# Cross attention with 16 dims per head: two heads' scores in bands of 32 rows, four heads turned per unit, normalisation moved to the output

## The chip, the cores and the metric

The kernel runs on one core of one Trainium2 chip. A core has a matmul engine (TensorE, PE in the profile; PEld is its weight load), a vector engine (VectorE, DVE), an activation engine (ScalarE, ACT), a general engine (GpSimd, POOL) and a queue for DMAs (SyncE, SP). Each engine runs its own list of instructions in order and waits on semaphores for the others. Matmuls write to PSUM, which has 8 banks of 2 KB in each of 128 partitions; everything else lies in SBUF. The metric is the device time of one execution in microseconds (us).

## The reference

Four small transformers are chained over the same stream x of shape (8, 112, 256): blocks of self attention, cross attention to a context of 375 tokens, and feed-forward layers (one of them a mixture of 8 experts). The change concerns the two cross attentions whose heads have 16 dims, in the first and the second transformer. Each of them computes, per batch element:

```
q = heads(norm(x) @ wq + bq)      # 16 heads x 112 x 16
k = heads(ctx @ wk + bk)          # 16 heads x 375 x 16
v = heads(ctx @ wv + bv)
s = einsum('bhqd,bhkd->bhqk', q, k) / 4
a = softmax(s, axis=-1)
o = einsum('bhqk,bhkd->bhqd', a, v)
x = x + merge(o) @ wo + bo
```

Everything is float32. The first transformer normalises the context as well.

## The kernel before

The program is a row of thirteen blocks. A cross block of this kind (`L0_ca`, `L1_ca`) works through the 8 batch elements. Ahead of the first element stands a prologue that makes its q, k and v; then comes one body per element, and a tail for the last one. The bodies of elements 1 to 6 are a loop over pairs. A body has 16 steps, and each step is one head, called a unit. In the body of element b the engines also make q, k and v of element b+1, in eight pieces: XT turns the normalised x, CT0 and CT1 turn the context, then come Q, K0, K1, V0 and V1. `SCHEDULES` gives, by hand, at which step PE does each piece (`plan`), at which step DVE and POOL do their parts (`dve`, `pool`), how many steps a head's probabilities are turned after its scores (`lag`), at which step the previous element's output is projected (`out_step`), and which PSUM banks the pieces, the scores and the turned probabilities use. A piece goes from PE to PSUM, and ACT takes it out to SBUF; ACT does so in its own list, behind the step's exponentials.

What happens to one head:

- `scores` (L683) multiplies q, masked to this head's 16 rows, with k: contraction over all 128 rows, 112 columns of weights, 375 moving columns. Two banks alternate. The masked q comes from `spread_q` on POOL (L497), eight masked copies for each half of the heads.
- `maxima` (L1243) takes the negative row maximum on DVE.
- `exps` (L975) writes exp(s - max) to one of four buffers in SBUF and sums the rows.
- `reciprocals` (L1248) inverts the sum on DVE; `scale` (L1530) multiplies the probabilities by it on POOL.
- `turn` (L696) transposes the 112 x 375 probabilities in three pieces of 125 columns on PE, `copy_turned` (L1257) copies them to SBUF on DVE.
- After four heads, `weigh` (L723) multiplies them with v: twelve matmuls whose weights are 32 columns wide, each head in its own 32 columns of the array.
- After sixteen heads, `evacuate` (L983) adds the value bias on ACT, `project` (L746) multiplies by wo, and `update` (L1289, L1290) adds the result to x.

One float32 matmul appears as two MATMUL records in the profile, one transposition as one.

## Time and profile before

| | us |
|---|---|
| median of 3 runs | 2317.31 |
| lowest and highest run | 2315.89, 2319.47 |
| the profiled execution, its own time | 2322.28 |
| its span, first to last instruction | 2320.4 |

The page of the profile gives for the whole span: PE busy 86%, its weight load 63%, DVE 70%, ACT 38%, POOL 36%. The two blocks in question lie at 139 to 375 us (`L0_ca`) and at 911 to 1145 us (`L1_ca`), together 20% of the span. The rest belongs to blocks that the change doesn't touch. Since the share of busy time is a mean over stages with different limits, the two blocks have to be read for themselves: the windows view gives busy time by stretch, and the view of instructions in order of time shows what follows what.

### The profile page before, as it was taken

To read this page: it belongs to the slowest core of one execution; us is meant where nothing else is said; L and a number is where in the kernel's file an instruction comes from. 1 tells how busy PE (TensorE), PEld (TensorE's weight loads), DVE (VectorE), ACT (ScalarE), POOL (GpSimd) and SP (SyncE) were. 2 spreads that over 40 slices of the span, in tenths; PEclk is the share of its full clock that TensorE was granted. 3 is DMA by queue.
4 is the path that set the end of the run, shared out by engine and by line. 5 is a ranking of instruction groups with operands and counts; after the bars stand their busy time and mean duration, and the time that the engine had idled before them with its cause. 6 is when DMAs were issued, how large, how long until landed. Compare 5 with 4: busy or idle time off the path is not lost.

```text
span 2320.4 us, 35838 instructions
## 1 busy us (share of the span) xinstructions
PE 2002.0 (86%) x11112; PEld 1464.4 (63%) x11112; DVE 1619.0 (70%) x3586; ACT 891.3 (38%) x2427; POOL 830.1 (36%) x950
## 2 busy tenths in 40 slices
PE   5879997999996877999888999685886968898878
PEld 4657776889895656777665555473444745565557
DVE  5856767677776876666665676595775958777765
ACT  4545553222222643555424444222331234444421
POOL 2235554666662233555420010041000424444433
PEclk9989998999997988999889999896997979999979
DMA  4100000211101000000100010101001000000100
GB/s 176 33 14 15 13 0 1 101 73 37 52 41 68 1 1 7 15 25 31 59 7 14 14 61 0 45 1 55 0 0 65 1 1 11 20 10 10 64 1 16
DMA packets 21631, 67.18 MB, mean 29 GB/s; under 512 B 880, under 2 KB 18568, under 8 KB 18832
## 3 DMA queue, kind: packets, MB, share of 16 engines
q1 hardware_dynamic: 21520, 65.78, 8.0%
q8 instruction: 59, 0.97, 0.2%
q14 instruction: 52, 0.43, 0.1%
HBM read 64.83 MB, written 0.95 MB: 28 GB/s over the span
## 4 chain that ended last, share of the span: by engine, by line
PE 60%; DVE 23%; issue 10%; ACT 3%; POOL 2%; DMA 1%; DVEq 0%; SPq 0%; POOLq 0%; ACTq 0%
PE ps L809 11%; PE ps L848 9%; PE ps L683 9%; PE ps L643 5%; PE ps L648 4%; PE ps L746 4%; PE ps L696 4%; PE ps L728 3%; PE ps L678 3%; POOL arena L1530 2%; PE ps L723 2%; PE ps L635 2%; DVE g_split_sb L1378 2%; DVE arena L1240 1%; DVE arena L1432 1%
## 5 line engine op out<-in xcount | busy, mean ns | idle before, releaser
L1530 POOL TENSOR_TENSOR arena<-arena,rinv 112x375 f32<-112x375 f32 (+1 forms) x448 | 372.0, 830 | 579.6 <-DVE rinv L1248 571.8
L683 PE MATMUL ps<-arena 128*112 128x375 f32 (+1 forms) x1280 | 387.5, 410 | 20.0 <-ACT arena L975 13.2
L809 PE MATMUL ps<-h_split_sb,w_split_sb 128*128 128x448 f32 x1536 | 355.5, 376 | 5.3 <-DVE h_split_sb L1368 4.3
L1559 POOL TENSOR_TENSOR w_split_sb<-wml,ones 128x256 fp32r<-128x256 f32 (+1 forms) x104 | 106.5, 1024 | 608.0 <-PE ps L809 396.6
L809 PEld LDWEIGHTS ps<-h_split_sb,w_split_sb 128*128 128x128 f32 x1536 | 298.4, 195 | 33.5 <-issue 5.9
L696 PEld LDWEIGHTS ps<-cst,arena 112*125 112x125 f32 (+1 forms) x1408 | 216.1, 183 | 156.5 <-POOL arena L1530 56.7
L848 PE MATMUL ps<-g_split_sb,w_split_sb 128*128 128x448 f32 x1248 | 292.9, 372 | 21.5 <-DVE g_split_sb L1378 21.1
L1243 DVE TENSOR_REDUCE negmax<-ps 112x1 f32<-112x375 f32 (+1 forms) x288 | 159.3, 553 | 159.2 <-PE ps L683 158.8
L848 PEld LDWEIGHTS ps<-g_split_sb,w_split_sb 128*128 128x128 f32 x1248 | 232.7, 189 | 55.6 <-DVE g_split_sb L1378 36.8
L975 ACT ACTIVATE arena<-ps,negmax 112x375 f32<-112x375 f32 (+1 forms) x384 | 190.5, 501 | 190.3 <-DVE negmax L1243 189.4
L696 PE MATMUL ps<-cst,arena 112*125 112x112 f32 (+1 forms) x1408 | 229.5, 275 | 38.6 <-POOL arena L1530 38.2
L683 PEld LDWEIGHTS ps<-arena 128*112 128x112 f32 x1280 | 176.7, 182 | 65.6 <-issue 24.6
L1377 DVE CAST g_split_sb<-arena 128x448 fp32r<-128x448 f32 x208 | 133.7, 643 | 112.6 <-PE ps L848 91.6
L975 ACT ACTIVATE arena<-arena,negmax 112x112 f32<-112x112 f32 (+1 forms) x256 | 125.8, 492 | 173.1 <-DVE negmax L1243 173.1
L1378 DVE TENSOR_TENSOR g_split_sb<-arena,g_split_sb 128x448 fp32r<-128x448 f32 x208 | 186.0, 894 | 7.1
L1257 DVE COPY arena<-ps 125x336 f32<-125x336 f32 x384 | 187.6, 488 | 2.3 <-PE ps L696 1.7
L643 PE MATMUL ps<-wat,arena 128*125 128x256 f32 (+1 forms) x704 | 175.7, 387 | 2.3 <-ACT arena L924 1.7
L1033 ACT ACTIVATE arena<-ps,wml 128x448 f32<-128x448 f32 x128 | 81.5, 637 | 233.6 <-PE ps L809 229.6
L643 PEld LDWEIGHTS ps<-wat,arena 128*125 128x125 f32 (+1 forms) x704 | 127.1, 188 | 33.9 <-issue 15.5
L746 PE MATMUL ps<-wat,arena 128*112 128x256 f32 x512 | 130.1, 402 | 14.6 <-DVE arena L1282 11.1
L1565 POOL TENSOR_TENSOR w_split_sb<-wml,ones 128x256 fp32r<-128x256 f32 x104 | 70.0, 673 | 194.5 <-PE ps L848 194.5
L1280 DVE RECIPROCAL arena<-ps 128x448 f32<-128x448 f32 x32 | 94.5, 2952 | 57.8 <-PE ps L734 57.8
(159 smaller groups left out, 3014.1 us busy)
## 6 DMA issues: line engine op xcount, KB each, us to landing
wml<-in_wm_L_moe SPq DMA_DIRECT2D x8, 2052.0 KB, 8.2
craw<-in_ctx SPq DMA_DIRECT2D x40, 375.0 KB
wml<-in_wm_L_m SPq DMA_DIRECT2D x3, 3072.0 KB, 14.0
wat<-in_wa_L_ca SPq DMA_DIRECT2D x2, 2560.0 KB, 9.4
wml<-in_wm_L_m SPq DMA_DIRECT2D x2, 2048.0 KB, 9.7
arena<-gates_hbm SPq DMA_DIRECT2D x1, 3584.0 KB, 11.0
wat<-in_wa_L_sa SPq DMA_DIRECT2D x1, 2560.0 KB, 8.8
wat<-in_wa_L_sa SPq DMA_DIRECT2D x2, 1024.0 KB, 9.6
```

The costliest lines, as they stand in the source:

```text
L643: last = mm(ps[0:blk.kp, W_BANK, i * D:(i + 1) * D], kv[:, k2, q * blk.kp:(q + 1) * blk.kp], w[:, k2], start=k2 == 0, stop=k2 == DC - 1)
L683: last = mm(ps[0:S, S_BANK + s % blk.s_banks, i * blk.nk:(i + 1) * blk.nk], qz[:, parity(b), head_of(u) if blk.dh == 16 else u], kT[:, par ...
L696: last = nc.tensor.transpose(ps[0:blk.kp, T_BANK + s % blk.t_banks, o:o + S], buf[:, i * blk.nk + q * blk.kp:i * blk.nk + (q + 1) * blk.kp ...
L746: last = mm(ps[0:S, blk.out_bank, 0:D], oT[:, c], wo[:, c], start=c == 0, stop=c == blk.cq - 1)
L809: last = mm(out, w[:, k2, v], h_split_sb[:, h, k2, tokens], start=k2 == 0 and i == 0, stop=k2 == DC - 1 and i == 2)
L848: last = mm(ACC(c, half), w[:, c * P:(c + 1) * P], g_split_sb[:, half, g], start=f == 0 and i == 0, stop=f == FC - 1 and i == 2)
L975: last = go(probs[0:S, s % blk.nprobs, i * nk:(i + 1) * nk], src[:, i * nk:(i + 1) * nk], ACT.Exp, bias=negmax[:, u:u + 1], accum_out=rows ...
L1243: v.tensor_reduce(negmax[:, s * blk.heads:(s + 1) * blk.heads], src, AX_X, ALU.max, negate=True).then_inc(maxed, 1)
L1257: last = v.tensor_copy(pT[0:kp, g % 4, :, s % HG], T_[:, 0:KC * S].rearrange("p (k s) -> p k s", s=S))
L1377: link(v.tensor_copy(g_split_sb[:, t % 2, 0], g32[:, t % 2]))
L1378: v.tensor_tensor(g_split_sb[:, t % 2, 1], g32[:, t % 2], g_split_sb[:, t % 2, 0].bitcast(F32), ALU.subtract)\
L1530: pool.tensor_tensor(p3, p3, r3, ALU.mult).then_inc(scaled, 1)
```

## The change

In both cross blocks with 16 dims per head (`blk.rows`):

- Scores. Two masked copies of q take the place of sixteen: one keeps the even group of 16 rows in each 32, the other the odd one (`maskz`). A head's scores are then a contraction over 32 rows, and `scores_of_rows` issues those of two heads, in two bands of 32 rows and to two banks, every second step. Four banks take scores where two did.
- `maxima_of_rows` reduces two heads with one instruction; eight take the place of sixteen.
- The probabilities stay unscaled. `scale` on POOL and fifteen of the sixteen `reciprocals` go. Eight buffers hold them where four did.
- `turn_rows` turns one third of four heads at a time (four transpositions of 125 columns into one bank), on three of every four steps; `keep_rows` copies 125 x 448. Twelve such units take the place of sixteen.
- `weigh` comes 10 steps after the head's step where it came 4 steps after.
- Normalisation at the output: `invert_rows` inverts the sixteen sums at once, `widen_shares` (POOL) spreads them to 16 columns each, `share` turns the result with two transpositions on PE, `keep_shares` copies it on ACT, `share_out` multiplies the output by it on DVE, `add_value_bias` adds the bias on POOL. They take the place of `evacuate`.
- The plan: the pieces move to other steps, and all of them go through PSUM bank 7 (`w_banks=[7]`), where three banks took turns. `out_step` goes from 6 to 11, `lag` from 3 to 6. `cnorm`, the context's norm in `L0_ca`, moves from step 2 to step 1 of DVE's list.

```diff
     "L0_ca": dict(
-        plan={2: ["XT"], 4: ["CT0"], 8: ["CT1"], 10: ["Q"], 12: ["K0"], 13: ["K1"], 14: ["V0"], 15: ["V1"]},
-        dve={0: ["norm"], 2: ["cnorm"]},
-        pool={12: ["spread0"], 14: ["spread1"]},
-        out_step=6, lag=3, s_banks=2, t_banks=2, w_banks=[7, 3, 2], out_bank=7),
+        plan={1: ["XT"], 2: ["CT0"], 3: ["CT1"], 5: ["Q"], 7: ["K0"], 9: ["K1"], 13: ["V0"], 15: ["V1"]},
+        dve={0: ["norm"], 1: ["cnorm"]},
+        pool={7: ["spread"]},
+        out_step=11, lag=6, s_banks=4, t_banks=2, w_banks=[7], out_bank=7),
...
+                def scores_of_rows(b, s):
+                    wait(pe, exped, count(st["unit"], units, b, s - 2))
+                    if s == 0:
+                        pe.wait_ge(spread, count(st["spread"], 1, b, 1))
+                        wait_evacuated(pe, blk, st, b, ["K0", "K1"])
+                    c, z = s // 8, s // 4 % 2
+                    for i in (s % 4, s % 4 + 1):
+                        rows = slice(32 * i, 32 * i + 32)
+                        mm(ps[0:S, S_BANK + i, 0:blk.nk], qzr[rows, parity(b), z, c], kT[rows, parity(b), c, 0:blk.nk],
+                           start=True, stop=True).then_inc(scored, 1)
+
+                def turn_rows(b, g, q):
+                    pe.wait_ge(exped, count(st["unit"], units, b, 4 * g + 4))
+                    wait(pe, row_kept, count(12 * st["row"], 12, b, 3 * g + q - 1))
+                    for i in range(4):
+                        last = nc.tensor.transpose(ps[0:blk.kp, T_BANK + (3 * g + q) % 2, i * S:(i + 1) * S],
+                                                   probs8[0:S, 4 * (g % 2) + i, q * blk.kp:(q + 1) * blk.kp], ident[0:S, 0:S])
+                    last.then_inc(row_turned, 1)
+
+                def share(b):
+                    pe.wait_ge(row_wide, count(st["row"], 1, b, 1))
+                    for c in range(DC):
+                        last = nc.tensor.transpose(ps[:, O_BANK, (DC + c) * S:(DC + c + 1) * S],
+                                                   rwide[:, parity(b), c * P:(c + 1) * P],
+                                                   ident[0:S, 0:S])
+                    last.then_inc(shares_full, 1)
...
+                        if at and blk.rows and at[1] % 4 < 3:
+                            turn_rows(at[0], at[1] // 4, at[1] % 4)
...
+                        due = lagged(b, s, WEIGH_AFTER, units)
+                        if blk.rows and due and due[1] % 4 == 0:
+                            weigh(due[0], due[1] // 4)
+                            if due[1] // 4 == 3:
+                                share(due[0])
...
+                    if blk.rows:
+                        act.wait_ge(row_maxed, count(8 * st["row"], 8, b, s // 2 + 1))
+                        wait(act, row_turned, count(12 * st["row"], 12, b, 3 * (s // 4 - 1)))
+                        go(probs8[0:S, s % 8, 0:nk], ps[0:S, S_BANK + s % 4, 0:nk], ACT.Exp, bias=negmax[:, s:s + 1],
+                           accum_out=rowsum[:, parity(b), s:s + 1]).then_inc(exped, 1)
+                        return
...
+                def keep_shares(b):
+                    act.wait_ge(shares_full, count(st["row"], 1, b, 1))
+                    go(shares, ps[:, O_BANK, DC * S:2 * DC * S], ACT.Copy).then_inc(shares_kept, 1)
...
+                def maxima_of_rows(b, s):
+                    dve.wait_ge(scored, count(st["unit"], units, b, s + 2))
+                    v.tensor_reduce(negmax[:, s:s + 2], ps[0:S, S_BANK + s % 4:S_BANK + s % 4 + 2, 0:nk], AX_X, ALU.max, negate=True)\
+                        .then_inc(row_maxed, 1)
...
+                def share_out(b):
+                    dve.wait_ge(shares_kept, count(st["row"], 1, b, 1))
+                    v.tensor_tensor(oT[:, 0:DC].rearrange("p c s -> p (c s)"), ps[:, O_BANK, 0:DC * S], shares, ALU.mult)\
+                        .then_inc(o_shared, 1)
...
-                        scale(b, s)
+                        if not blk.rows:
+                            scale(b, s)
```

Where it moves things, at two places of the loop body. PE's list of `L0_ca` before, at steps 3 to 5 (L683 scores, L696 turn, L723 weigh, L623 the piece CT0):

```order
259 L683 MATMUL ps<-arena 112x375 [waits exped]
260 L696 MATMUL ps<-cst,arena 125x112 [waits turned,scaled]
261 L696 MATMUL ps<-cst,arena 125x112 x2
262 L723 MATMUL ps<-arena,vz 32x112 [waits turned]
263 L723 MATMUL ps<-arena,vz 32x112 x11
...
269 L618 REGISTER_ALU [waits w_done1]
270 L623 MATMUL ps<-cst,arena 128x125 [waits cn_ready]
```

The same list after the change, at steps 2 and 3 (L707 scores of two heads, L715 turn, L768 weigh, L631 the pieces CT0 and CT1):

```order
238 L707 MATMUL ps<-arena 112x375 [waits exped]
239 L707 MATMUL ps<-arena 112x375
...
241 L715 MATMUL ps<-cst,arena 125x112 [waits row_kept]
242 L715 MATMUL ps<-cst,arena 125x112 x3
...
245 L768 MATMUL ps<-arena,vz 32x112 x11
...
247 L626 REGISTER_ALU [waits w_done0]
248 L631 MATMUL ps<-cst,arena 128x125 [waits cn_ready]
...
250 L715 MATMUL ps<-cst,arena 125x112 [waits row_kept,exped]
...
253 L631 MATMUL ps<-cst,arena 128x125 [waits cn_ready,w_done0]
```

CT1 now follows CT0 by one unit of turning, and waits for the bank that CT0 is in (`w_done0`); before, four steps and another bank lay between.

DVE's list of `L0_ca` before, at steps 2 and 3 (L1243 maxima, L1248 reciprocals, L1257 copies, L1116 the context's norm):

```order
259 L1243 TENSOR_REDUCE negmax<-ps 112x1 [waits scored]
260 L1248 RECIPROCAL rinv<-rowsum 112x1 [waits exped]
261 L1257 COPY arena<-ps 125x3x112 [waits av_done,transposed]
...
265 L1116 TENSOR_SCALAR arena<-craw,ctx_mean,ctx_rstd_ln 125x256
...
271 L1243 TENSOR_REDUCE negmax<-ps 112x1 [waits scored]
```

The same list after, at steps 0 to 2 (L1315 maxima, L1320 the sixteen reciprocals, L1326 copies, L1184 both norms):

```order
210 L1315 TENSOR_REDUCE negmax<-ps 112x2 [waits scored]
...
212 L1320 RECIPROCAL rinv<-rowsum 112x2x2x4 [waits exped]
...
215 L1326 COPY arena<-ps 125x448 [waits av_done]
...
219 L1184 TENSOR_SCALAR xn<-X,mv,rstd 112x256
...
223 L1184 TENSOR_SCALAR arena<-craw,ctx_mean,ctx_rstd_ln 125x256
...
229 L1315 TENSOR_REDUCE negmax<-ps 112x2 [waits scored]
```

The norm of x, the three instructions of the context's norm and the reciprocals now stand in one row between the maxima of the first two pairs of heads; before, two maxima lay between the two norms.

## Rows read from the trace of the kernel before

**Rows 1.** The page: the whole span.
```profile
span 2320.4 us, 35838 instructions
```
**Rows 2.** Windows: length; busy us of PE, PEld, DVE, ACT, POOL; granted clock; DMA.
```profile
139.80:149.60 9.80, 9.42 (x37) 7.43 (x38) 0.84 (x3) 4.48 (x10) 3.33 (x2) 0.73 0.13 39
149.60:175.90 26.30, 24.87 (x181) 17.36 (x180) 16.48 (x48) 15.17 (x43) 15.52 (x17) 1.00 0.05 16
175.90:340.90 165.00, 163.23 (x1298) 118.70 (x1297) 113.76 (x330) 93.27 (x270) 97.48 (x108) 1.00 0.03 10
340.90:370.40 29.50, 24.70 (x214) 16.98 (x212) 21.64 (x74) 12.11 (x37) 16.39 (x22) 0.94 0.01 2
912.30:921.20 8.90, 8.88 (x36) 7.40 (x37) 0.00 (x0) 4.00 (x10) 3.33 (x2) 0.76 0.14 43
947.00:1111.80 164.80, 161.94 (x1298) 117.86 (x1297) 106.67 (x312) 92.67 (x270) 97.22 (x108) 1.00 0.07 23
```
**Rows 3.** Groups by line and shape in 175.9:340.9: count, busy us, mean ns, idle before.
```profile
L683 PE MATMUL ps<-arena 128*112 128x375 f32 x193 | 80.4, 497 | 1.8 <-ACT arena L975 1.3
L975 ACT ACTIVATE arena<-ps,negmax 112x375 f32<-112x375 f32 x96 | 55.1, 574 | 57.5 <-DVE negmax L1243 57.1
L1243 DVE TENSOR_REDUCE negmax<-ps 112x1 f32<-112x375 f32 x96 | 52.2, 544 | 47.7 <-PE ps L683 47.6
L1257 DVE COPY arena<-ps 125x336 f32<-125x336 f32 x96 | 46.8, 487 | 0.0
```
**Rows 4.** PE in order of time, L0_ca: start, duration to the last end, line, shape.
```profile
241.51 0.48 PE L696 MATMUL ps<-cst,arena 112*125 112x112 f32 x3
241.91 0.78 PE L723 MATMUL ps<-arena,vz 125*32 125x112 f32 x24
242.63 0.88 PE L683 MATMUL ps<-arena 128*112 128x375 f32 x2
243.35 0.48 PE L696 MATMUL ps<-cst,arena 112*125 112x112 f32 x3
...
243.99 0.80 PE L683 MATMUL ps<-arena 128*112 128x375 f32 x2
244.62 0.48 PE L696 MATMUL ps<-cst,arena 112*125 112x112 f32 x3
```
**Rows 5.** PE in order of time, L3_ca: 448 columns, weights 64 wide, two heads together.
```profile
2071.35 2.48 PE L728 MATMUL ps<-arena,vz 125*64 125x448 f32 x12
```
**Rows 6.** Groups by line and shape, whole span: DVE copies 448 columns out of PSUM.
```profile
L1259 DVE COPY arena<-ps 112x448 f32<-112x448 f32 x64 | 38.5, 601 | 4.2 <-PE ps L696 4.0
```
**Rows 7.** ACT in order of time, prologue of L1_ca: CT0 and CT1, Q.
```profile
913.64 1.06 ACT L926 ACTIVATE arena<-ps 128x375 f32<-128x375 f32 x2
915.90 0.60 ACT L914 ACTIVATE qs<-ps,cst 128x112 f32<-128x112 f32 x2 [1.20 <-PE ps L628]
```
**Rows 8.** The tail of L0_ca in order of time: last scores, last project.
```profile
364.50 0.80 PE L683 MATMUL ps<-arena 128*112 128x375 f32 x2
...
370.40 2.04 PE L746 MATMUL ps<-wat,arena 128*112 128x256 f32 x4 [0.72 <-ACT arena L983]
```
**Rows 9.** DVE in order of time, L0_ca: norm of x, norm of the context.
```profile
232.78 0.72 DVE L1116 TENSOR_SCALAR xn<-X,mv,rstd 112x256 f32 x1
235.32 1.32 DVE L1116 TENSOR_SCALAR arena<-craw,ctx_mean,ctx_rstd_ln 125x256 f32<-125x256 f32 x3
```
**Rows 10.** PE in order of time, L3_ca: two idle times, then 512 columns.
```profile
2064.55 0.41 PE L613 MATMUL ps<-cst,xn 112*128 112x112 f32 x2 [1.07 <-DVE xn L1115]
...
2066.80 3.67 PE L648 MATMUL ps<-wat,arena 128*112 128x512 f32 x4 [0.89 <-ACT arena L918]
...
2073.75 1.97 PE L648 MATMUL ps<-wat,arena 128*112 128x512 f32 x4
```
**Rows 11.** Windows of L3_ca, columns as in rows 2.
```profile
2062.90:2066.80 3.90, 1.94 (x11) 1.32 (x10) 3.83 (x10) 1.89 (x6) 1.62 (x2) 1.00 0.44 136
2066.80:2070.50 3.70, 3.70 (x5) 1.52 (x6) 1.88 (x6) 0.70 (x2) 0.81 (x1) 0.54 0.00 1
```

More of the change, by code:

```diff
@@ L177, in starts @@
             at["unit"] += B * blk.units
[L178 to L179 removed]
+            at["turn"] += B * blk.units * (not blk.keys_first and not blk.rows)
+            at["row"] += B * blk.rows
+            at["spread"] += B * blk.rows
             at["pair"] += B * 2 * blk.keys_first
```

117 lines of the change are left out of this document (86 added, 31 removed).

## The prediction

> **What bounds the kernel now.** The windows come first, since the two blocks that change are a fifth of the span [rows 1]. For each of them they separate a prologue, a first body, six steady bodies and the last body with its tail [rows 2]. In the steady stretch of L0_ca PE is busy 163.2 of 165.0 us at the full granted clock, DVE 113.8, ACT 93.3, POOL 97.5. L1_ca reads the same: 161.9 of 164.8. So a body of 27.5 us (165.0 / 6) is bound by PE, and POOL's multiplications, though many, wait for others. Next comes PE in order of time [rows 4]. The reader is to take pitches there, from one start to the next, since a matmul's end is modelled. A head's scores take 0.63 us (243.99 to 244.62), or 0.72 where the 32-column matmuls stand ahead of them (242.63 to 243.35). Three transpositions take 0.32 us (243.35 to 243.67, the row left out there being CT0), or 0.40 when those matmuls follow (241.51 to 241.91). Four groups of four 32-column heads are not drawn out: 24 records of 112 columns pass in 0.72 us (241.91 to 242.63).
>
> **PE, per steady body.** Out go the scores of 16 heads, 12 at 0.63 and 4 at 0.72: 10.4 us, 10.7 with the short waits in the loop's first steps. In come 8 pairs, whose price the trace doesn't hold, since nothing runs in bands of rows yet. Its bounds: side by side, a pair streams for as long as one head, 0.63 us; one after the other, for 1.26 us. To either belongs the passage between forms. From full width into 32-column tiles costs 0.40 - 0.32 = 0.08 us; out of them, the last groups' pitch and the slow first load cost about 0.09 + 0.09 us [rows 4]. A pair has a passage in, 112 columns to load that nothing hides (0.09, the 0.72 against 0.63), and a passage out with the next load open: about 0.36 us. So a pair costs between 0.63 (all of it hidden) and 1.62 us, and I take 0.63 + 0.36 = 1.0 us. The reason is the nearest row: in L3_ca two heads in 64-column halves pass 12 records of 448 columns in 2.40 us, 0.20 us each, where a head's score record of 375 columns alone takes 0.315 us, which is 0.376 us for 448 [rows 4, 5]. Halves of columns run side by side at 0.20 / 0.376 = 0.53, almost two at once, though each matmul's two records follow each other in the list. Bands of rows are the same kind of split. Eight pairs at 1.0 make 8.0 us: a gain of 2.7.
>
> The Trainium skill (TensorEngine Tiling (Array Packing), Key Properties) says that changing the tiling mode drains the engine. The 0.08 us in and the 0.09 us out agree, for columns; no row here shows it for bands. The same skill (TensorE: Matmul & The Clock Gate, Measured speedup vs the span model) has four bands reach 3.07 times, and by that two would come close to two.
>
> The 48 transpositions remain: 0.107 us each (0.32 / 3). With four passages into the weighing it is 5.5 us before and after. Weighing keeps its matmuls, but each of its four ends now falls on transpositions with an open load, 4 x 0.09 = 0.4 us more; before, that stood in the 0.72 of the scores. `share` adds two transpositions, 0.25 us. The waits on exponentials at the loop's start go, since four score banks take the place of two: a gain between 0 and 0.6 us, I take 0.3. Sum: -2.7 + 0.4 + 0.25 - 0.3 = -2.35, a body of 25.1 us if no engine makes PE wait.
>
> **The others, per body.** DVE has 8 maxima of 750 elements. 375 take 0.544 us; copies of 336 and 448 take 0.487 and 0.601, so an element more costs 1.02 ns, and 750 take 0.544 + 0.38 = 0.93 [rows 3, 6]. Its 12 copies of 448 cost 0.60 [rows 6] for 16 of 0.487 [rows 3]; the reciprocals shrink to one. `share_out` costs about 0.4. DVE falls from 19.0 (113.8 / 6) to about 16: -1.3 for the maxima, -0.6 for the copies, about -1.2 for the reciprocals (their overlap taken off), +0.4. ACT keeps 16 exponentials of 0.574, swaps one evacuation for another: no change. POOL loses 16 multiplications; its spread of q is one instruction of 448 elements. None of this bounds, so what POOL loses is worth nothing in the bodies; PE's work hides it.
>
> **The new wait.** All pieces go through bank 7, and XT, CT0 and CT1 stand at steps 1, 2 and 3. I lay the body's start out, with 0 at the first pair's start. In L1_ca: first maxima 1.05 to 2.0, two exponentials to 3.1, XT out of the bank at 3.8. DVE meanwhile does reciprocals, a copy and the norm of x (0.72) [rows 9] up to 3.3, and only then the maxima of the second pair, to 4.2. Exponential 2 ends at 4.8, and behind it in ACT's list CT0 leaves the bank at 5.3. PE arrives at CT1 at 4.65 and waits 0.7 us; queued behind it are the next pair and a turn. In L0_ca the context's norm (1.32) [rows 9] stands ahead of the second maxima too. They end at 5.4, CT0 leaves at 6.6, and PE waits about 2.0 us, 0.6 of it for `cnorm` itself. After that no wait of the hand-laid body bites: the exponentials of a group are 2 to 3 us ahead of its turning, and the bias on POOL (o_done) is 2 us ahead of `project`. Bodies: 25.1 + 0.7 = 25.8 in L1_ca, 25.1 + 2.0 = 27.1 in L0_ca. Six of each: 6 x (27.5 - 25.8) = 10.2 and 6 x (27.5 - 27.1) = 2.4 us of gain.
>
> **The edges.** In the prologue, 9.8 and 8.9 us [rows 2], the pieces overlapped over three banks. Now each of seven waits until ACT has taken the one before out: 0.53 for each context half, 0.60 for Q [rows 7], and so on, with about 0.15 until a matmul's end is seen. 7 x 0.75 = 5.3, to which cold clock adds a little and from which what was exposed already (XT) goes: +5.5 us per block, between 4 and 8. POOL's spread, 3.3 us before [rows 2], was hidden behind K and V and its saving is worth nothing. First body: no weighing of an element before, four banks: -1.8 in L1_ca, -1.0 in L0_ca. Last body and tail: 29.5 us from its first scores to the last `project` (340.9 to 370.4), the last 5.9 of them behind the start of the last scores [rows 8]. The tail grows: the last four heads go through three turns and copies, weighing, `share`, ACT, DVE and POOL, about 3 us more than one turn, one copy and ACT. The body has no pieces, so DVE leads there, with some 3 us less to do; laid out by hand the same way it comes to 28.3. That is -1.2 us per block.
>
> **The sum.** L1_ca: -10.2 - 1.8 - 1.2 + 5.5 = -7.7. L0_ca: -2.4 - 1.0 - 1.2 + 5.5 = +0.9. I add 0.8 for register work around the new waits that the hand-laid body leaves out: -6.0 us. The profiled execution took 2322.3 us (its span 2320.4), which becomes 2316.3; it lies 5.0 above the median of the runs, so the forecast is 2317.3 - 6.0 = **2311.3 us**. The span of this case: each 0.1 us on a pair is worth 128 pairs x 0.1 = 12.8 us over both blocks, so it reaches from 2298 to 2322.
>
> **Rivals.**
> *The passage costs nothing.* If weights of a band load while the other computes, a pair costs 0.8 us: -0.2 x 128 = -26 us, **2286**. For it: bands need not share rows with the load that comes next. Against: the 0.08 and 0.09 of the column tiles [rows 4].
> *The waits at CT0 and CT1 slow the clock (slower than before).* In L3_ca PE idles 1.07 and 0.89 us within 3.9 us [rows 10, 11], and the 512 columns behind that run at the lower of the two clocks (granted 0.54): 3.67 us for what takes 1.97 at full clock, +1.7. L0_ca's new wait has the same form: 2.0 us idle in about 4, with transpositions around it. Seven bodies x 1.7 = 12, and as much again in waits where ACT is behind: -6 + 12 = +6, **2323**, up to 2338. It decides from about 1 us of idle in L1_ca, 2 in L0_ca. For it: every granted-clock row of both blocks is 1.00 only because PE never waits. Against: in both blocks PE's idle time would come in two parts, around CT0, and each is shorter than 1.4 us.
> *The pair doesn't run side by side.* Each head's two records go one after the other: 1.62 per pair, +0.62 x 128 = +79 us, **2391**. Against it: rows 5, at 0.53.
> Of POOL's 97.5 us per stretch nothing comes back in any of these.
>
> **How the numbers follow.** Forecast 0.45, free passage 0.17, slow clock and waits 0.29, no pair 0.09. About 0.2% (4.6 us) is what a measurement of this kernel can tell from no change. Of the forecast's 0.45 I give 0.25 to faster, 0.14 to the band, 0.06 to slower, since its size hangs on the pair's price; of the slow clock 0.06 to the band and 0.23 to slower. Faster 0.25 + 0.17 = 0.42; same 0.20; slower 0.06 + 0.23 + 0.09 = 0.38. The range goes from 2288, the free passage but for its far end, to 2338, the top of the waits; beyond it lie the missing pair and tails, under 0.2.
>
> **What would show it.** In the changed profile: pitch from a pair's start to the turn behind it of 1.0 us (0.8: free passage; 1.6: no pair). Idle of PE ahead of the CT pieces, ended by ACT, of 0.7 us a body in L1_ca and 2.0 in L0_ca. A maximum of 0.93. Prologue of 15 us in place of 9.8. Steady stretches of about 155 us (L1_ca) and 163 (L0_ca), at granted clock 1.00. A clock under 1.00 there, or PE waiting for maxima or row_kept in the middle of a body, would make the prediction wrong; so would a change in any other block.

## The result: 3.8% slower, most of it at TensorE's lower clock

The changed kernel took 2407.56 us (median of 4 runs, 2394.78 to 2430.24), the kernel before 2318.39 us beside it (4 runs). The ratio is 1.038, with a 95% interval of 1.0336 to 1.0425. The forecast was 2311.3 us with a range of 2288 to 2338. So the sign was wrong, and the time lies far outside the range. The profiled execution took 2419.89 us, its span is

```profile
span 2418.0 us, 34738 instructions
```

against the 2320.4 of [rows 1]: 97.6 us more. I cut both spans at the turning of x (XT) of elements 0, 1 and 7 and at the last `project` of each block. The table has the lengths in us, and those of some experiments below.

| | before | after | e1 | e6 | e8 |
|---|---|---|---|---|---|
| L0_ca, XT of element 0 to XT of element 1 | 12.6 | 22.5 | 20.9 | 10.9 | 11.7 |
| L0_ca, six bodies, to XT of element 7 | 164.1 | 184.1 | 157.5 | 157.7 | 165.9 |
| L0_ca, to the last `project` | 53.8 | 58.1 | 54.9 | 49.2 | 52.8 |
| L1_ca, XT of element 0 to XT of element 1 | 13.2 | 22.2 | 20.6 | 9.8 | 9.6 |
| L1_ca, six bodies, to XT of element 7 | 164.4 | 203.5 | 154.5 | 154.9 | 161.2 |
| L1_ca, to the last `project` | 51.4 | 62.2 | 54.9 | 48.6 | 52.2 |

After against before: 18.9 us went into the two prologues, 59.1 into the bodies, 15.1 into the ends, and 4.5 outside these pieces. The windows view of the changed kernel (columns as in [rows 2]) shows what the stretches have in common:

```profile
138.40:158.60 20.20, 15.01 (x38) 8.56 (x38) 0.82 (x3) 4.51 (x10) 0.93 (x1) 0.53 0.06 20
948.40:967.00 18.60, 13.91 (x32) 7.89 (x32) 0.00 (x0) 4.02 (x10) 0.93 (x1) 0.52 0.07 21
1002.90:1208.00 205.10, 197.80 (x1315) 127.20 (x1316) 98.69 (x156) 86.21 (x265) 12.31 (x18) 0.75 0.06 18
```

The steady stretch of L1_ca ran at a granted clock of 0.75 where [rows 2] had 1.00. PE was busy for 197.8 us of it, and only 161.9 before, though it has less to do. A view of instructions in order of time, on PE, shows the point at which the clock falls in each of those bodies:

```profile
1034.14 0.89 PE L707 MATMUL ps<-arena 32*112 32x375 f32 x4
1034.95 0.69 PE L715 MATMUL ps<-cst,arena 112*125 112x112 f32 x4
1037.10 0.41 PE L621 MATMUL ps<-cst,xn 112*128 112x112 f32 x2 [1.46 <-DVE xn L1184]
1037.44 1.07 PE L707 MATMUL ps<-arena 32*112 32x375 f32 x4
1038.44 1.18 PE L715 MATMUL ps<-cst,arena 112*125 112x112 f32 x4
...
1052.63 2.66 PE L643 MATMUL ps<-arena,wat 128*128 128x375 f32 x4
1055.22 0.89 PE L707 MATMUL ps<-arena 32*112 32x375 f32 x4
```

At 1034.14 four records of scores take 0.89 us and four turns 0.69: the upper of the two levels (2.4 GHz). Then PE stands idle for 1.46 us, until the norm of x is there. The turns behind it take 1.18 us, the lower level (1.2 GHz), and it stays there until the K piece at 1052.63. After that the upper level is back, for the second half of the body, until XT comes round again. DVE in the same stretch shows why the norm is late:

```profile
1035.10 0.94 DVE L1315 TENSOR_REDUCE negmax<-ps 112x2 f32<-112x750 f32 x1 [1.10 <-PE ps L707]
1035.95 0.24 DVE L1320 RECIPROCAL rinv<-rowsum 112x16 f32<-112x16 f32 x1
1036.11 0.56 DVE L1326 COPY arena<-ps 125x448 f32<-125x448 f32 x1
1036.59 0.45 DVE L1184 TENSOR_SCALAR xn<-X,mv,rstd 112x256 f32 x1
```

DVE was free for 1.10 us. But it works its list in order, and the norm stands behind the maxima of the first pair, which wait for PE. The waits view of the six bodies of L1_ca has this one wait and no other:

```profile
PE ps L621 <- DVE xn L1184: 8.8, 6, 1.5
```

### The profile page after: what moved, and what is told of

The parts are those of the page before. It is cut to its first block, busy times and chain, and to the rows that moved or that the text cites. A ratio compares the mean times of both kernels' runs of the same rounds, so it can differ in the third digit from the quotient of the medians.

```text
span 2418.0 us, 34738 instructions
## 1 busy us (share of the span) xinstructions
PE 2064.0 (85%) x11144; PEld 1468.6 (61%) x11144; DVE 1595.4 (66%) x3170; ACT 874.8 (36%) x2411; POOL 610.9 (25%) x710
## 4 chain that ended last, share of the span: by engine, by line
PE 62%; DVE 22%; issue 10%; ACT 3%; POOL 2%; DMA 1%; DVEq 0%; SPq 0%; POOLq 0%; ACTq 0%
PE ps L863 10%; PE ps L902 9%; PE ps L715 5%; PE ps L707 5%; PE ps L651 5%; PE ps L656 4%; PE ps L791 4%; PE ps L773 3%; PE ps L688 3%; PE ps L768 2%; PE ps L643 2%; PE ps L693 2%; POOL arena L1633 2%; DVE arena L1308 2%; DVE g_split_sb L1477 2%
## 5 line engine op out<-in xcount | busy, mean ns | idle before, releaser
L1633 POOL TENSOR_TENSOR arena<-arena,rinv 112x375 f32<-112x375 f32 (+1 forms) x192 | 163.9, 854 | 388.4 <-DVE rinv L1336 388.4
L1315 DVE TENSOR_REDUCE negmax<-ps 112x2 f32<-112x750 f32 x128 | 119.9, 937 | 194.0 <-PE ps L707 193.9
L1027 ACT ACTIVATE arena<-ps,negmax 112x375 f32<-112x375 f32 x256 | 144.5, 568 | 193.9 <-DVE negmax L1315 174.8
L693 PE MATMUL ps<-arena 128*112 128x112 f32 (+1 forms) x768 | 173.3, 351 | 10.0 <-ACT arena L1011 5.5
L715 PEld LDWEIGHTS ps<-cst,arena 112*125 112x125 f32 x768 | 123.7, 232 | 87.6 <-issue 83.6
L1326 DVE COPY arena<-ps 125x448 f32<-125x448 f32 x192 | 118.3, 616 | 72.2 <-PE ps L715 70.5
L715 PE MATMUL ps<-cst,arena 112*125 112x112 f32 x768 | 157.0, 339 | 0.0
L736 PEld LDWEIGHTS ps<-cst,arena 112*125 112x125 f32 (+1 forms) x640 | 90.9, 174 | 83.5 <-POOL arena L1633 53.2
L736 PE MATMUL ps<-cst,arena 112*125 112x112 f32 (+1 forms) x640 | 104.5, 279 | 37.3 <-POOL arena L1633 37.2
L707 PE MATMUL ps<-arena 32*112 32x375 f32 x512 | 134.7, 607 | 0.0
```

The source lines that it names most:

```text
L693: last = mm(ps[0:S, S_BANK + s % blk.s_banks, i * blk.nk:(i + 1) * blk.nk], qz[:, parity(b), head_of(u) if blk.dh == 16 else u], kT[:, par ...
L707: mm(ps[0:S, S_BANK + i, 0:blk.nk], qzr[rows, parity(b), z, c], kT[rows, parity(b), c, 0:blk.nk], start=True, stop=True).then_inc(scored, 1)
L715: last = nc.tensor.transpose(ps[0:blk.kp, T_BANK + (3 * g + q) % 2, i * S:(i + 1) * S], probs8[0:S, 4 * (g % 2) + i, q * blk.kp:(q + 1) * ...
L736: last = nc.tensor.transpose(ps[0:blk.kp, T_BANK + s % blk.t_banks, o:o + S], buf[:, i * blk.nk + q * blk.kp:i * blk.nk + (q + 1) * blk.kp ...
L1027: go(probs8[0:S, s % 8, 0:nk], ps[0:S, S_BANK + s % 4, 0:nk], ACT.Exp, bias=negmax[:, s:s + 1], accum_out=rowsum[:, parity(b), s:s + 1]).t ...
L1633: pool.tensor_tensor(p3, p3, r3, ALU.mult).then_inc(scaled, 1)
```

## Experiments 1 to 4: idle time, or bands?

Two theories stood against each other. IDLE: PE's wait for XT lowers the clock. BANDS: matmuls over 32 of the 128 rows don't hold the clock up, whether PE waits or not. (In diffs and in rows of a trace, `...` stands for lines left out.) The median of the kernel before, over 11 runs beside these, was 2317.79 us.

**e1: the norm of x ahead of the first maxima on DVE.**

```diff
-                        if s == 0 and more(b) and blk.keys_first:
+                        if s == 0 and more(b) and (blk.keys_first or blk.rows):
                             extra("norm", b + 1, link)
...
-                                if name != "norm" or not blk.keys_first:
+                                if name != "norm" or not (blk.keys_first or blk.rows):
```

> The changed kernel, with the norm of x for the next element moved ahead of the first maxima in DVE's list of a body, so that PE doesn't idle 1.46 us at XT. Theory IDLE (PE's idle time at XT is what lowers the clock): granted clock of the steady bodies back to 0.97 or more, PE alternating no longer between its two levels, time 2310 to 2325 us. Theory BANDS (matmuls over 32 of 128 rows don't hold the clock, whatever the idle time): the steady bodies still spend about half their time at the lower level, and only the idle time goes, 14 x 1.5 = 20 us: about 2387 us.

Measured: 2332.1 us (6 runs), ratio 1.0061 (1.0041 to 1.0081): 7 us above the range of IDLE, and 55 below the number of BANDS. Moving one instruction of 0.40 us gave back 75 of the 89 us. On PE and in the windows view, the same place of L1_ca:

```profile
1040.86 0.69 PE L715 MATMUL ps<-cst,arena 112*125 112x112 f32 x4
1041.39 0.36 PE L621 MATMUL ps<-cst,xn 112*128 112x112 f32 x2
1041.67 0.89 PE L707 MATMUL ps<-arena 32*112 32x375 f32 x4
```

```profile
213.30:316.80 103.50, 99.88 (x875) 63.90 (x874) 68.57 (x117) 57.45 (x176) 8.29 (x12) 1.00 0.03 11
1016.00:1041.40 25.40, 25.05 (x222) 16.06 (x221) 16.25 (x27) 14.00 (x44) 2.07 (x3) 1.00 0.05 15
```

The bodies take 25.9 us (103.5 / 4) in L0_ca and 25.3 in L1_ca, at clock 1.00, with bands. So bands alone don't lower it here.

**e2: the kernel before, each head's scores over its own band of 32 rows**, one head at a time, the masked copies as they were.

```diff
+                        band = slice(32 * (u % 4), 32 * (u % 4) + 32) if blk.dh == 16 and blk.cross else slice(0, P)
                         last = mm(ps[0:S, S_BANK + s % blk.s_banks, i * blk.nk:(i + 1) * blk.nk],
-                                  qz[:, parity(b), head_of(u) if blk.dh == 16 else u],
-                                  kT[:, parity(b), u // 8, 0:blk.nk], start=True, stop=True)
+                                  qz[band, parity(b), head_of(u) if blk.dh == 16 else u],
+                                  kT[band, parity(b), u // 8, 0:blk.nk], start=True, stop=True)
```

> The kernel before, with each head's scores contracted over its band of 32 rows instead of 128 (the same masked q, one head at a time, nothing else changed). PE stays busy without idle time, each score pays the passage into and out of the band. IDLE: granted clock stays at 1.00 in the steady bodies; each head costs about 0.3 us more, 256 x 0.3 = 75 us: about 2390 us. BANDS: the clock falls to 0.85 or less in the steady bodies, and the time to 2440 us or more.

Measured: 2635.09 us (2 runs), ratio 1.1374. BANDS said 2440 us or more, and this is far above that edge; IDLE said 2390. PE in order of time in L0_ca, first at the upper level, then at a place of a later body where the level falls; and the windows view of four later bodies:

```profile
152.92 0.88 PE L684 MATMUL ps<-arena 32*112 32x375 f32 x2
153.73 0.58 PE L697 MATMUL ps<-cst,arena 112*125 112x112 f32 x3
154.24 0.88 PE L684 MATMUL ps<-arena 32*112 32x375 f32 x2
...
242.69 0.58 PE L697 MATMUL ps<-cst,arena 112*125 112x112 f32 x3
...
244.33 0.97 PE L697 MATMUL ps<-cst,arena 112*125 112x112 f32 x3
245.23 1.35 PE L724 MATMUL ps<-arena,vz 125*32 125x112 f32 x24
246.51 1.59 PE L684 MATMUL ps<-arena 32*112 32x375 f32 x2
248.03 0.97 PE L697 MATMUL ps<-cst,arena 112*125 112x112 f32 x3
```

```profile
195.50:385.90 190.40, 190.40 (x867) 105.36 (x866) 81.09 (x221) 64.09 (x180) 65.17 (x73) 0.64 0.03 9
```

PE was busy for all 190.4 us, without a single wait, and was granted 0.64. At the upper level a head and its turn take 1.32 us (0.81 + 0.51, from the pitches), against 0.95 in [rows 4]; at the lower one 2.4 (1.52 + 0.90). So a busy PE isn't enough: with one band of 32 rows at work at a time the clock falls without any idle time, again in each of these bodies.

The Trainium skill (TensorE: Matmul & The Clock Gate, Loop structure matters more than you think) says that matmuls stay at the higher clock when they are issued densely, back to back. These rows speak against that as a sufficient rule.

**e3: the changed kernel, scores over all 128 rows**, from sixteen masked copies, the layout and the late norm as changed.

```diff
-                        rows = slice(32 * i, 32 * i + 32)
-                        mm(ps[0:S, S_BANK + i, 0:blk.nk], qzr[rows, parity(b), z, c], kT[rows, parity(b), c, 0:blk.nk],
+                        mm(ps[0:S, S_BANK + i, 0:blk.nk], qz[:, parity(b), 8 * c + 2 * i + z], kT[:, parity(b), c, 0:blk.nk],
...
```

POOL spreads q to the sixteen copies, as before the change.

> The changed kernel, with sixteen masked copies of q and scores over all 128 rows, one head after the other, everything else as changed (plan, lags, banks, idle time at XT). IDLE: the clock alternates as in the changed kernel (0.68 and 0.82 in turns), the scores cost 0.3 us more a pair at full clock: 2420 to 2460 us. BANDS: granted clock 1.00 in the steady bodies in spite of the idle time, time 2335 to 2360 us.

Measured: 2372.19 us (2 runs), ratio 1.0239, 12 us above the range of BANDS and 48 below that of IDLE. The waits and windows views of L1_ca:

```profile
PE ps L621 <- DVE xn L1183: 8.1, 5, 1.6
```

```profile
1013.80:1042.70 28.90, 27.14 (x218) 19.74 (x218) 16.21 (x26) 14.19 (x45) 4.47 (x4) 1.00 0.04 15
```

The wait for XT is there, 1.6 us in each body, and the clock is 1.00 all the same. A body takes 28.9 us and not 34.2.

**e4: the kernel before, XT at step 0**, so that PE waits for the norm.

```diff
-        plan={2: ["XT"], 4: ["CT0"], 8: ["CT1"], 10: ["Q"], 12: ["K0"], 13: ["K1"], 14: ["V0"], 15: ["V1"]},
+        plan={0: ["XT"], 4: ["CT0"], 8: ["CT1"], 10: ["Q"], 12: ["K0"], 13: ["K1"], 14: ["V0"], 15: ["V1"]},
...
-        plan={3: ["XT"], 5: ["CT0"], 6: ["CT1"], 9: ["Q"], 12: ["K0"], 13: ["K1"], 14: ["V0"], 15: ["V1"]},
+        plan={0: ["XT"], 5: ["CT0"], 6: ["CT1"], 9: ["Q"], 12: ["K0"], 13: ["K1"], 14: ["V0"], 15: ["V1"]},
```

> The kernel before, with XT in step 0 of the body in both cross blocks, where it has to wait for the norm of x: 1 to 2 us of idle PE in each body, scores over 128 rows, nothing else changed. IDLE: the granted clock of the steady bodies falls to 0.9 or less, time 2360 us or more. BANDS: the clock stays at 1.00, and only the idle time is paid, 14 x 1.7 = 24 us: about 2340 us.

Measured: 2334.97 us (4 runs), ratio 1.0086. The waits and windows views of L1_ca:

```profile
PE ps L613 <- DVE xn L1116: 7.2, 5, 1.4
```

```profile
1010.00:1038.60 28.60, 26.99 (x216) 19.65 (x216) 17.89 (x52) 15.55 (x45) 16.20 (x18) 1.00 0.04 13
```

A body grows by 1.1 us, about the new wait, and the clock stays at 1.00.

Together the four give a table, for L1_ca but for e2 (L0_ca):

| scores | PE hardly waits | PE waits 1.4 to 1.6 us in a body |
|---|---|---|
| all 128 rows | 1.00 (before) | 1.00 (e3, e4) |
| 32 rows, two bands side by side | 1.00 (e1) | 0.75 (after) |
| 32 rows, one band at a time | 0.64 (e2) | not run |

Neither theory was right alone. With bands side by side the clock stays up as long as PE hardly waits, and a wait that costs the other kernels no more than itself takes it down. The price in L1_ca: a body of 34.2 us, against 25.3 in e1 plus the wait of 1.46, is 7.5 us more. In L0_ca the same wait of 1.46 us stands in every body, and they take between 28.2 and 34.3 us, where e1 has 25.9 with 0.9 of waits: 2 to 8 us beyond the wait. A pair of bands also brings two passages between forms of matmul, and none of the kernels that wait has the one without the other; e9 below separates them only for a PE that doesn't wait.

## Experiment 7: another way to take the wait away

**e7: the changed kernel, XT, CT0, CT1 and Q at steps 3, 4, 5 and 6**, in both blocks.

```diff
-        plan={1: ["XT"], 2: ["CT0"], 3: ["CT1"], 5: ["Q"], 7: ["K0"], 9: ["K1"], 13: ["V0"], 15: ["V1"]},
+        plan={3: ["XT"], 4: ["CT0"], 5: ["CT1"], 6: ["Q"], 7: ["K0"], 9: ["K1"], 13: ["V0"], 15: ["V1"]},
```

> The changed kernel with nothing but the hand layout altered: XT, CT0, CT1 and Q at steps 3, 4, 5 and 6 of the body and not at 1, 2, 3 and 5. The norm of the next element stays behind the first maxima on VectorE. Its XT was waited for 1.46 us at step 1; two steps later a pair of scores and turns of some 2.1 us lie ahead of it on TensorE. Theory IDLE: the wait of 1.46 us is what lowers the clock; with it gone the bodies come to 25.5 to 26.5 us at clock 1.00 as in e1, and the time to 2325 to 2340 us. Theory ORDER: e1 was faster for what moved on VectorE and not for TensorE's wait; then the bodies stay at 28 to 34 us and the time at 2390 us or more.

Measured: 2373.88 us (3 runs), ratio 1.0237. Both numbers missed; the bodies of L1_ca lie in the range of ORDER, the time between the two. PE in order of time in L1_ca:

```profile
1047.35 0.36 PE L621 MATMUL ps<-cst,xn 112*128 112x112 f32 x2
...
1049.08 0.54 PE L631 MATMUL ps<-cst,craw 125*128 125x125 f32 x3
1050.74 0.54 PE L631 MATMUL ps<-cst,craw 125*128 125x125 f32 x3 [1.13 <-ACT arena L980]
1051.21 1.59 PE L707 MATMUL ps<-arena 32*112 32x375 f32 x4
```

XT is no longer waited for. In its place CT1 waits 1.13 us for bank 7, which CT0 still fills, since nothing lies between the two at the new steps. The scores behind that wait are at the lower level again (1.59 for 0.89). The bodies of L1_ca come to 28.3 and 29.6 us in turn. The wait moved and the fall moved with it, which speaks for IDLE; that the loss is smaller here fits the shorter wait and the shorter stay at the lower level. In L0_ca two waits of 0.78 and 0.76 us stand in every body; two of the bodies kept granted clock 1.00 and took 27.4 us, the other three were granted 0.84 to 0.94 and took 28.9 to 31.3.

## Experiments 5 and 6: the prologue and the end

e1 still lay 14 us behind the kernel before, 11.3 in the profiled executions. The table shows 16 us in the prologues and 5 in the ends, 4 more than its bodies gain; the other 7.5 lie outside the two blocks (see e11).

**e5: e1, and the pieces of element 0 over several banks.** PE and ACT take the bank from a list of its own where `m` is 0, and PE waits for the evacuation that it needs, no longer for the last one.

```diff
+        self.first_banks = [7, 3, 2, 7, 3, 2, 7, 6] if self.rows else None
...
+                    if first:
+                        W_BANK = blk.first_banks[k]
+                        needs = {"Q": ["XT"], "K": ["CT1"], "V": ["CT1"]}.get(name[0], [])
+                        same = [j for j in range(k) if blk.first_banks[j] == W_BANK] + [blk.pieces.index(x) for x in needs]
+                        wait(pe, done, value - 1 - k + max(same + [-1]) + 1)
...
```

> The kernel of e1 (the norm ahead of the first maxima), and the eight pieces of element 0, ahead of the first body, written to banks 7, 3, 2, 7, 3, 2, 7, 6 in turn and not all to bank 7. e1 took 2332.1 us, and its stretch ahead of the first body 21.0 us in L0_ca and 20.7 us in L1_ca, against 9.8 and 8.9 us in the kernel before. Theory ONE BANK: the stretch is long because each piece waits for the evacuation of the last, and its clock is low because of those waits. Then it comes back to some 10.5 us, and the first body (28.1 us, clock 0.82) to some 26.5: 2332 - 2 x 10.4 - 2 x 1.6 = 2308 us. Theory LOW CLOCK: the clock is at its lower level there for another reason, and only the waits go (21.0 us less the 15.8 us that TensorE is busy): 2332 - 2 x 5.2 = 2322 us.

Measured: 2309.92 us (7 runs), ratio 0.996 (0.9946 to 0.9975), the kernel before at 2320.33 us beside it. First the changed kernel's prologue, PE in order of time, then that of e5:

```profile
139.92 0.86 PE L631 MATMUL ps<-cst,arena 125*128 125x125 f32 x3 [0.92 <-ACT arena L972]
141.53 0.89 PE L631 MATMUL ps<-cst,arena 125*128 125x125 f32 x3 [0.76 <-ACT arena L978]
143.18 2.05 PE L636 MATMUL ps<-arena,wat 128*128 128x112 f32 x8 [0.76 <-ACT arena L978]
145.91 2.87 PE L643 MATMUL ps<-arena,wat 128*128 128x375 f32 x4 [0.69 <-ACT qs L968]
```

```profile
140.40 1.48 PE L640 MATMUL ps<-cst,arena 125*128 125x125 f32 x6 [0.36 <-DVE arena L1195]
141.68 1.89 PE L645 MATMUL ps<-arena,wat 128*128 128x112 f32 x8
143.36 3.23 PE L652 MATMUL ps<-arena,wat 128*128 128x375 f32 x8
```

With one bank there are seven waits of 0.66 to 0.92 us, and all of the work stands at the lower level (a K piece of 2.87 us takes 1.44 in a steady body). With several banks the waits go but for one of 0.36 us, the prologue takes 9.7 us (139.43 to 149.11), and over it the granted clock is 0.74, where it was 0.53. ONE BANK was right; only the first body, which was to get 1.6 us shorter, stayed at 28.3.

**e6: e5, and the statistics for the next block taken once, at the end.** Before and after the change, DVE takes them for elements 0 to 6 in the last body, in a row of 3.5 us, and for element 7 at the very end. The end of that row in e1, on DVE, with eleven more small ones between the second and the third line, and then on PE:

```profile
356.39 0.58 DVE L1199 BATCH_NORM_AGGREGATE mv<-stat 112x2 f32<-112x6 f32 x7
357.00 0.17 DVE L1205 TENSOR_SCALAR var<-mv 112x7 f32<-112x7 f32 x1
...
359.42 0.94 DVE L1315 TENSOR_REDUCE negmax<-ps 112x2 f32<-112x750 f32 x1
```

```profile
360.94 1.11 PE L768 MATMUL ps<-arena,vz 125*32 125x112 f32 x24 [3.10 <-DVE arena L1326]
361.98 3.14 PE L715 MATMUL ps<-cst,arena 112*125 112x112 f32 x12
```

```diff
-                                statistics(tail, n + 1, 0 if b == B - 1 else B - 1, b)
+                                if not blk.rows:
+                                    statistics(tail, n + 1, 0 if b == B - 1 else B - 1, b)
+                                elif b == B:
+                                    statistics(tail, n + 1, 0, B)
```

> The kernel of e5, and the statistics of the residual for the next block taken once, for all eight elements behind the last update, and not for seven of them at step 11 of the last body and for the eighth at the end. In e1 TensorE stood idle for 3.1 us at 357.8 us, behind those statistics on VectorE, and went on at the lower clock (12 turns in 3.14 us for some 1.9). Theory TAIL: both go, in both blocks: 3.1 us of idle time, some 2 us of slow turns, weighings and projection, less some 0.5 us for seven more aggregations at the end: some 4.6 us for each block, e5 less 9 us, and 2299 us if e5 is 2308. Theory VECTORE BOUND: VectorE is the bound of the last body anyway, and only the work saved comes back (some 3 us of small instructions less 0.5, of which half is hidden): e5 less 2 to 3 us.

Measured: 2293.32 us (4 runs), ratio 0.9875 (0.9853 to 0.9898), 1.2% faster than the kernel before. The gain over e5 is 16.6 us, more than TAIL's 9. In the profiled executions the last part of a block falls from 56.0 and 54.8 us (e5) to 49.2 and 48.6, 13 in all; the whole span falls by 12.2. The twelve turns are at the upper level:

```profile
348.10 2.15 PE L724 MATMUL ps<-cst,arena 112*125 112x112 f32 x12
```

## Experiments 8 to 11: what the bands are worth, and what is not theirs

The kernel before stood at 2319.43 us over 18 runs beside these.

**e8: e6 with the scores over all 128 rows** (the diff of e3).

> The kernel of e6 (2293.3 us), with each head's scores computed over all 128 rows from 16 masked copies of the queries, as in e3: the bands alone are taken out, everything else stays. TensorE has hardly a wait in the bodies of e6 (25.3 us, clock 1.00). Theory SIDE BY SIDE: two heads in bands of their own save TensorE time at the full clock: in e3 a body was 28.9 us of which 1.6 us were the wait for XT, so 27.3 us, 2.0 us more than in e6; over 16 bodies 32 us: 2325 us. Theory CLOCK ONLY: what bands save, they lose in the first bodies and the ends, which run at the lower clock in e6 (0.82 in the first) and would not here: 2.5 us in each of two first bodies come back, and 2320 us. If the bands save nothing, it stays at 2293 us.

Measured: 2315.34 us (7 runs), ratio 0.9981 (0.9961 to 1.0), some 5 us below the lower of the two numbers. With hardly a wait in the way the bands save 22 us. A steady body takes 27.8 us in L0_ca and 27.2 in L1_ca, 1.9 more than in e6, as SIDE BY SIDE had it (2.0); the first bodies give part of that back, as CLOCK ONLY had it. The table above has 8.2 and 6.3 us of it in the bodies and 3.6 in either end; the rest lies outside the two blocks or in the spread of single executions. The first body is shorter in e8 by 1.4 us (L0_ca) and 3.0 (L1_ca), since its clock is 0.94 and 1.00 there and 0.82 in e6.

**e9: the kernel before, each head's scores over 64 rows**, as e2 but for

```diff
+                        half = slice(64 * (u % 4 // 2), 64 * (u % 4 // 2) + 64) if blk.dh == 16 and blk.cross else slice(0, P)
```

> The kernel before, with each head's scores over the 64 of the 128 rows that hold it, where e2 took 32: 2635 us at a mean clock of 0.834, and TensorE without a wait. Theory THE MORE ROWS REST, THE LOWER: the clock lies between, some 0.9, and the time at 2400 to 2500 us. Theory ONLY BANDS OF 32: 64 rows hold the full level as 128 do; then the time is that of before plus what the passages from half to full rows cost (two for each of 256 heads at some 0.05 to 0.1 us: 25 to 50 us), 2340 to 2370 us, or 2318 us if they cost nothing.

Measured: 2416.2 us (one run), in the first theory's range, but not in its way. The windows view:

```profile
183.30:247.10 63.80, 63.80 (x434) 36.42 (x433) 38.60 (x111) 31.35 (x90) 32.47 (x37) 1.00 0.04 14
967.90:1013.30 45.40, 45.40 (x214) 24.62 (x213) 18.78 (x52) 15.80 (x46) 17.28 (x20) 0.66 0.03 9
```

The steady bodies keep clock 1.00, and take 31.9 us for 27.5. That is the passages: a head and its turn take 1.32 us as in e2, against 0.95 in [rows 4], so 0.37 us for two passages, where the expectation had 0.1 to 0.2. Twelve heads a body have no weighing behind them that would bring a passage anyway: 12 x 0.37 = 4.4. Only the first body of L1_ca fell to 0.66 and took 45.4 us; a wait of 1.01 us stands 2 us ahead of it. So half the rows hold the level nearly everywhere where a quarter (e2) did not. Since a head and its turn have the same passages in both, the passages are not what takes the clock in e2.

**e10: e6 with its own plan for the first body**, CT0, CT1, Q, K0 and K1 at steps 3, 5, 7, 9 and 11.

```diff
+        self.plan0 = {1: ["XT"], 3: ["CT0"], 5: ["CT1"], 7: ["Q"], 9: ["K0"], 11: ["K1"], 13: ["V0"], 15: ["V1"]} if self.rows else self.plan
...
-                            for name in blk.plan.get(s, []):
+                            for name in (blk.plan0 if isinstance(b, int) and b == 0 else blk.plan).get(s, []):
```

> The kernel of e6, with a hand layout of its own for the first body of either attention, in which no turns lie between the pieces: CT0, CT1, Q, K0 and K1 at steps 3, 5, 7, 9 and 11 and not at 2, 3, 5, 7 and 9. In e6 TensorE waited 1.83 and 0.76 us there for CT0 and CT1, fell to the lower clock for 10 us, and the body took 28.3 us for 25.9. Theory: the waits go and with them the fall, 2.4 us in each block: 2293.3 - 4.8 = 2288.5 us. Rival: XT, CT0 and CT1 are waited for because ScalarE comes to them late, behind the exponentials, and wait again at the new steps: 2293 us.

Measured: 2297.0 us (5 runs), ratio 0.9903 (0.9888 to 0.9919): no gain over e6. The wait of 1.83 us for CT0 stayed in the first body, as the rival said; the one for CT1 fell from 0.76 to 0.34 and the body from 28.3 to 27.7. More telling is a later body of L0_ca in the profiled execution:

```profile
203.50:210.00 6.50, 5.60 (x54) 3.69 (x53) 4.92 (x10) 4.33 (x12) 0.62 (x1) 0.94 0.17 48
210.00:220.00 10.00, 10.00 (x54) 6.55 (x54) 3.03 (x5) 3.65 (x12) 0.00 (x0) 0.53 0.02 7
234.10:260.00 25.90, 25.00 (x220) 16.00 (x220) 17.11 (x30) 14.34 (x44) 2.07 (x3) 1.00 0.04 15
```

All steady bodies of L0_ca in e1, e5, e6 and e10, twenty in all, have the same two waits, 0.2 us for CT0 and 0.7 for CT1. This one fell to the lower level behind them and took 30.7 us; the one that starts at 234.1 did not. So with bands even 0.9 us of waits can be followed by a fall, once in twenty here.

**e11: the kernel before with the one edit of e6**, its statistics taken once in the two blocks.

```diff
-                                statistics(tail, n + 1, 0 if b == B - 1 else B - 1, b)
+                                if not (blk.dh == 16 and blk.cross):
+                                    statistics(tail, n + 1, 0 if b == B - 1 else B - 1, b)
+                                elif b == B:
+                                    statistics(tail, n + 1, 0, B)
```

> The kernel before, with the one edit of e6 that is not bound to the change: the statistics for the next block taken once at the end of the two cross attentions with 16 dims. Before, TensorE waits 2.95 us at 355.8 us behind them. What it gives here is to be subtracted from the gain of e6. Theory TAIL: the wait goes in both blocks, less 0.4 us of aggregations at the end: 2318 - 2 x 2.5 = 2313 us. Theory VECTORE BOUND: VectorE is the last body's bound and little comes back: 2317 us.

Measured: 2321.49 us (10 runs), ratio 1.0003 (0.9991 to 1.0016). The edit does what TAIL says inside the blocks: their ends take 49.3 and 46.9 us for 53.8 and 51.4, 9 us in all. But the profiled execution has the span of before to the tenth. The way back lies in L3_ca, which no edit touched. On DVE, in order of time:

```profile
2014.94 0.55 DVE L1240 TENSOR_TENSOR arena<-ps,mask_sb 112x375 f32<-112x375 f32 x1 [4.43 <-issue]
...
2018.14 0.35 DVE L1115 TENSOR_SCALAR xn<-X,rstd 112x256 f32 x1 [1.60 <-issue]
```

DVE stands for 4.43 and 1.60 us, and the profile names nothing that it waits for. PE then waits 6.64 us for the norm, and a body of 43.4 us takes 47.8; a later one loses 4.5. Outside the two blocks e11 takes 9.0 us more than before, which eats up the gain.

The other traces show when this happens. The changed kernel, e1, e3, e5, e7 and e11 have two such stops of DVE in L3_ca, 3.75 to 4.73 us each and one pass of the loop over pairs of elements apart. Before, e2, e4, e6, e8, e9 and e10 have none. The DMA view of e11 in 1990:2019, around the stop, has a queue that the same stretch of before doesn't have:

```profile
q14 instruction: 4, 0.03, 0.3%
```

In each of the twelve stops a packet of this queue begins. In the seven kernels without stops it moves nothing for at least 140 us of L3_ca. So the stops go together with the loading of instructions inside that loop, though no edit touched that block; that the loading causes them is likely, but no run tests it. What they cost differs: L3_ca, from the turning of x of its third element to that of its eighth, takes 7.4 us longer in e11 than before, but only 0.5 longer in e5 than in e6.

So the gain of e6 isn't owed to them: neither it nor the kernel before has a stop. In the profiled executions e6 is 28.5 us shorter than before within the two blocks and 3.0 longer outside. Within the blocks, e8 (all of e6 but the bands) is 6.1 us shorter than before, and e11, with the edit of the statistics alone, 9.0. The bands bring 22.4; the rest of the change, without that edit, costs some 3 us. Against e11, e6 is 28 us faster; in the profiled executions 19.5 us lie in the blocks and 6.0 outside.

## Why the prediction was wrong, point by point

**What bounded the kernel** was read rightly: PE, at the upper level, with nothing to spare in the other engines that counts. That "every granted-clock row of both blocks is 1.00 only because PE never waits" stood in the text under a rival. The rows themselves had 0.73, 0.76 and 0.94 at the edges of the blocks [rows 2]; only the bodies had 1.00. And e4 corrects the reason: before, PE could wait 1.4 us a body and keep 1.00.

**The price of a pair** was right. Forecast 1.0 us. In e6 and e1 it is 0.82 us to the turn behind it (1040.05 to 1040.86). The turn is 0.62 us where a pair follows and 0.53 where a full-width piece does, so 0.09 for the passage in. And 0.53 is 0.10 more than four transpositions at the 0.107 us of [rows 4], for the passage out. Together 1.01, of which 0.38 are the two passages (forecast 0.36; e9 has 0.37). e8 confirms it by another way: 1.9 us a body are 0.24 a pair, and two heads at 0.63 less 1.01 are 0.25. This term, on which the range hung, was the firm one.

**The step that failed is "The new wait".** The hand-laid body had the norm of x on DVE end at 3.3 us, and XT leave its bank at 3.8. PE comes to XT at 1.5 us: one pair and one unit of turns. The layout took XT as ready there and began to look for waits at CT1. The wait was in its own numbers, 3.3 - 1.5 = 1.8 us, and measured it is 1.46 (DVE ended at 2.9). By itself it is worth 14 x 1.46 = 20 us, and 2311.3 + 20 would still lie in the range. The rest is what it brings with it, the fall of the clock, which the sum put at nothing. With the wait, the 0.7 us in front of CT1 is gone in L1_ca, since PE arrives later. The rows of DVE's list after the change showed the norm of x behind the first maxima. I used them for the second maxima, and didn't ask who waits for the norm itself.

**The clock rival** had the right mechanism and the wrong place and size. It was put at CT0 and CT1 in L0_ca. It came at XT, in both blocks, most in L1_ca. It was priced at 1.7 us a body, from a stretch of L3_ca in which the level came back after 3.7 us of full-width matmuls. Here, behind the wait, come scores in bands, turns of 112 columns and weighings, and in L1_ca the level stayed down for some 17 us (1038.4 to 1055.2): 7.5 us a body. That the kind of work behind the wait makes it so long is not shown: in L0_ca the same list gave bodies of 28.2 and of 34.3 us. "About 1 us of idle in L1_ca" as the point from which it decides was near, 1.13 us in e7 did; "2 in L0_ca" was too high, 1.46 did.

**Bodies without that wait** came to 25.9 and 25.3 us (e1), against forecasts of 27.1 and 25.8. So the gain would have been 1.6 and 2.2 us a body. In L0_ca the waits were overrated, 0.9 us for 2.0.

**Prologue**: forecast +5.5 us, measured +10.4 and +9.7 (20.2 and 18.6 us). The waits were right, seven of 0.66 to 0.92. "Cold clock adds a little" was the mistake: with a wait behind each piece all of it ran at 0.52, half as fast as in a steady body.

**First and last body**: forecast -1.8, -1.0 and -1.2 for the end; e1 has 28.1 us in the first, 1.5 us (L0_ca) and 1.0 (L1_ca) more than before, and its ends are 1.1 and 3.5 longer. In both, a wait (1.83 us for CT0, 3.10 for the statistics) is followed by turns and weighings at the lower level. The last body's row of statistics cost 2.95 us of waiting before too; it wasn't in the rows that I read.

**DVE** went as forecast: maxima of 0.94 for 0.93, copies of 0.62 for 0.60. That POOL's work comes back as nothing no run tests alone; e8, which has lost it as well, keeps within 0.2% of before.

The chance of 0.38 for slower was fair; the range was not. Its upper end, 2338, was some 14 bodies at 1.7 us (which make 2335). At 7.5 us each the same rival gives 2311 + 14 x 7.5 = 2416, and 2407.56 was measured; but that they are so close is luck. The six bodies of L0_ca lost 26.6 us against e1 and those of L1_ca 49.0, waits included, and of the 97.6 us against before only 59.1 came in bodies. Another 34.0 came in the prologues and ends, for which the sum has 11.0 and a gain of 2.4. The other span of the text slipped as well: 12.8 us on either side of 2311.3 reach to 2324, not 2322.

## What to carry to other kernels

When a layout is drawn by hand, go through PE's list first and ask of every entry what it needs and where that stands in the other engine's list. The new wait was of one cheap instruction, queued behind one that waits for PE itself. When work is made narrower, the granted clock becomes part of its price: look for every wait that was harmless before, the ends and the prologue too, and take them away together with the change. And price a fall of the clock by the time that the level stays down, not by the wait: the same 1.46 us cost from 2 to 8 us beyond themselves.

## What the runs showed of the hardware that I had not expected

- PE busy without a pause can be granted 0.64: one head's scores over 32 rows, in turn with transpositions and weighings (e2). Over 64 rows it was 1.00 but for one body (e9), and with two bands of 32 side by side 1.00 in the steady bodies as long as the waits of a body came to 0.9 us or less (e1, e5, e6), with one exception (e10).
- A wait of 1.4 to 1.6 us costs itself with full rows (e3, e4) and 2 to 8 us more with bands (after), 7.5 in each body of L1_ca. The Trainium skill (TensorE: Matmul & The Clock Gate, A second HAM failure mode: psum-queue depth-cycling) describes short idle times between groups of matmuls that make the clock go to and fro. The changed kernel agrees with that, 0.75 on the mean of L1_ca; e3 and e4 show that idle time of the same length need not do it.
- Why L0_ca after the change kept much of its clock while L1_ca lost it in every body (184.1 and 203.5 us for the same six bodies) stays open; the wait of 1.46 us is the same in all of them.
- VectorE can stand for 4 us in a block that no edit touched, in step with packets of the instruction queue. Six of the thirteen kernels have it and seven don't; in e11 it went with 9.0 us outside the blocks, as much as the edit gained inside them.
